# VectorE's program of a graph layer as one lap written out and two loops

## The reference

```
agg = segment_sum(edge_attr, dst, nodes)          # 200000 edges x 128, dst sorted, 6250 nodes
h   = relu(concat([x, agg, u], 1) @ W1 + b1)       # u: one row of 64, for all nodes
y   = x + h @ W2 + b2
out = (y - mean(y)) / sqrt(var(y) + 1e-5)          # over the 128 features of a node
```

## Time and profile before

| | us |
|---|---|
| median of 3 runs | 287.8 (287.53 to 287.91) |
| the profiled execution | 288.01 |
| its span, first to last instruction | 286.2 |
| outside the span | 1.8 |
| PE busy | 204.1 (71%) |
| DVE busy | 159.7 (56%) |
| ACT busy | 46.5 (16%) |
| POOL busy | 43.9 (15%) |
| bytes moved by DMA | 110.05 MB |

### The profile page before, as it was taken

One profiled execution on the slowest core, in us unless ns is written; L12 is line 12 of the kernel. 1 busy time (PEld: TensorE's weight loads), 2 busy tenths in 40 slices (PEclk: granted clock), 3 DMA queues, 4 the chain that ended last, 5 costly groups with the idle time before them and its releaser, 6 DMA issues.

```text
span 286.2 us, 11430 instructions
## 1 busy us (share of the span) xinstructions
PE 204.1 (71%) x4997; PEld 159.5 (56%) x4997; DVE 159.7 (56%) x422; ACT 46.5 (16%) x98; POOL 43.9 (15%) x49
## 2 busy tenths in 40 slices
PE   0567699786796697687946855956877668656782
PEld 0455587655575576566635644645555555545671
DVE  3983565764655754844864365274345454785522
ACT  0411032211220221212102101120111121110100
POOL 8200020210400400400421021040021040030020
PEclk9995999999999999999997999898979977997957
DMA  7999999999999999999999999999999999999991
GB/s 178 352 377 401 401 398 400 402 401 401 402 400 402 400 399 404 400 401 404 399 399 402 398 402 401 401 401 401 400 401 400 403 401 399 398 400 397 403 394 59
DMA packets 40092, 110.05 MB, mean 385 GB/s; under 512 B 2485, under 2 KB 3658, under 8 KB 40074
## 3 DMA queue, kind: packets, MB, share of 16 engines
q1 hardware_dynamic: 37012, 105.85, 95.9%
q10 hardware_dynamic: 3062, 3.99, 4.2%
HBM read 106.63 MB, written 3.20 MB: 384 GB/s over the span
## 4 chain that ended last, share of the span: by engine, by line
PE 47%; DMA 34%; issue 13%; DVE 3%; ACT 0%; SPq 0%; POOLq 0%; DVEq 0%; POOL 0%
DMA slots<-in_edge_attr 33%; PE rows_ps L738 26%; PE cols_ps L750 12%; PE hid_ps L782 2%; PE hid_ps L764 2%; DMA dst_int<-in_dst 2%; PE hid_ps L773 2%; PE hid_ps L758 1%; DVE low L505 1%; DVE edge_node L521 1%; PE rows_ps L723 1%; DVE z L608 0%; ACT rows L383 0%; PE hid_ps L858 0%; DVE dst_local L510 0%
## 5 line engine op out<-in xcount | busy, mean ns | idle before, releaser
L738 PE MATMUL rows_ps<-slots,hot 64*32 64x128 f32 (+1 forms) x4560 | 110.9, 286 | 59.3 <-issue 45.7
L738 PEld LDWEIGHTS rows_ps<-slots,hot 64*32 64x32 f32 (+1 forms) x4560 | 92.4, 112 | 76.0 <-issue 75.4
L570 DVE TENSOR_TENSOR agg_t<-agg_t,cols_ps 128x128 f32 (+1 forms) x65 | 21.7, 334 | 108.1 <-PE cols_ps L750 107.9
L551 DVE TENSOR_TENSOR hot<-edge_node,iota 128x768 f32<-128x768 f32 x65 | 61.9, 952 | 6.3 <-issue 6.3
L750 PE MATMUL cols_ps<-row_hot,rows 128*128 128x224 f32 (+1 forms) x190 | 48.5, 365 | 7.3 <-ACT rows L383 7.0
L383 ACT ACTIVATE rows<-rows_ps 128x128 f32<-128x128 f32 (+1 forms) x65 | 21.2, 326 | 190.7 <-PE rows_ps L738 186.9
L351 POOL TENSOR_TENSOR rstd<-var_eps,minus_half 128x4 f32<-128x4 f32 (+1 forms) x13 | 19.9, 1532 | 203.7 <-DVE var_eps L602 203.7
L750 PEld LDWEIGHTS cols_ps<-row_hot,rows 128*128 128x128 f32 x190 | 33.0, 200 | 21.5 <-ACT rows L383 12.8
L342 POOL TENSOR_TENSOR z<-x_rows,b_all 128x512 f32<-128x512 f32 (+1 forms) x13 | 16.2, 1250 | 35.5 <-PE hid_ps L758 35.2
L560 DVE TENSOR_TENSOR row_hot<-row_node,iota 128x448 f32<-128x448 f32 x30 | 19.6, 654 | 0.0
L608 DVE TENSOR_SCALAR z<-z,moments,rstd 128x128 f32<-128x128 f32 x49 | 18.6, 438 | 1.6 <-POOL rstd L351 1.6
(11 more groups left out here) (97 smaller groups left out, 65.4 us busy)
## 6 DMA issues: line engine op xcount, KB each, us to landing
slots<-in_edge_attr SPq DMA_DIRECT2D x65, 1536.0 KB, 18.6
x_rows<-in_x ACTq DMA_DIRECT2D x11, 256.0 KB
out<-z SPq DMA_DIRECT2D x11, 256.0 KB
dst_int<-in_dst SPq DMA_DIRECT2D x2, 192.0 KB, 4.2
dst_int<-in_dst ACTq DMA_DIRECT2D x2, 192.0 KB, 4.0
x_rows<-in_x ACTq DMA_DIRECT2D x1, 192.0 KB
out<-z SPq DMA_DIRECT2D x1, 192.0 KB
rest_slot<-in_edge_attr ACTq DMA_DIRECT2D x1, 160.0 KB, 8.8
```

The costliest lines, as they stand in the source:

```text
L551: V.tensor_tensor(hot[i][:, :, :], edge_node[:, bass.ds(t, 1), :, :].rearrange("p o c r -> p (o c r)").unsqueeze(2).broadcast_to([P, RUNS, ...
L570: V.tensor_tensor(cols, cols, cols_ps[:, 0:n], ALU.add).then_inc(added, 1)
L738: done = T.matmul(rows_ps[i][c * SPAN:(c + 1) * SPAN, h, 0:feats], hot[j][part, c * RUN + r, :], slots[part, j, c, r * feats:(r + 1) * fea ...
```

## The change

Only VectorE's program is written in another way. Lap 0 stays written out. Laps 1 to 5 become one loop (`Fori(1, DENSE_LAP)`) over `sparse_lap`, laps 6 to 12 a second (`Fori(DENSE_LAP, laps)`) over `dense_lap`. The lap's number is now a register, and so are addresses and wait values that hang on it. What only some laps do stands in `dve.If`:

- in a sparse lap, the `row_hot` for the steps t + 3 of j = 2, 3, 4 is the sparse or the dense form by two `If`, since those of lap 5 belong to lap 6;
- in a dense lap, `hot` and `row_hot` of j = 2, 3, 4 are made only where there is a lap to come; `judge` and `make_plan` stand in an `If` each.

`make_plan` stands now after `variance` of step j = 2 of the last lap; before, it stood at the end of step j = 1. `variance` waits at two places for `ids_copied` where its register form waited for `plan_made`; both are semaphores that have long been set where this is run. `edge_node` and `row_node` are longer by three steps, which are addressed but not used.

```diff
-        edge_node = sb("edge_node", [P, steps, TILES, RUN])
-        row_node = sb("row_node", [P, steps, HALVES])
+        edge_node = sb("edge_node", [P, steps + AHEAD, TILES, RUN])
+        row_node = sb("row_node", [P, steps + AHEAD, HALVES])
...
-                if dense_step:
+                make_row_hot(t, i, dense_step)
+
+            def make_row_hot(t, i, dense_step):
+                if dense_step is None:
+
+                    with dve.If(t < DENSE):
+                        make_row_hot(t, i, False)
+                    with dve.If(t > DENSE - 1):
+                        make_row_hot(t, i, True)
+                elif dense_step:
...
-                    dve.wait_ge(plan_made, 1)
+                    dve.wait_ge(ids_copied, CHUNKS)
...
-            def lap_of(lap):
-                at = step_bases(lap * LAP, LAP)
+            def counts(lap):
+
+                for j in range(-1, LAP + AHEAD + 1):
+                    dve.compute_val(lap * LAP + j)
+                for n in range(2):
+                    dve.compute_val(lap + n)
+                return step_bases(lap * LAP, LAP)
+
+            def sparse_lap(lap):
+                at = counts(lap)
                 for j in range(LAP):
                     t = lap * LAP + j
-                    if t + AHEAD < steps:
-                        make_hot(t + AHEAD, j + AHEAD, t + AHEAD >= DENSE)
-                    add(t, at[j], t >= DENSE)
-
-                    k = j + 1 if lap >= DENSE_LAP else j
-                    if lap and k == 2:
+
+                    mixed = not isinstance(lap, int) and j + AHEAD >= LAP
+                    make_hot(t + AHEAD, j + AHEAD, None if mixed else False)
+                    add(t, at[j], False)
+                    if isinstance(lap, int):
+                        continue
+                    if j == 2:
                         residual(lap - 1, lap - 1)
-                    elif lap and k == 3:
+                    elif j == 3:
                         variance(lap - 1, lap - 1)
-                    elif lap and k == 4:
+                    elif j == 4:
                         normalise(lap - 1, lap - 1)
-                    if t == (laps - 2) * LAP + 1:
-                        judge()
-                    elif t == (laps - 1) * LAP + 1:
-                        make_plan()
+
+            def dense_lap(lap):
+                at = counts(lap)
+                for j in range(LAP):
+                    t = lap * LAP + j
+                    if j + AHEAD < LAP:
+                        make_hot(t + AHEAD, j + AHEAD, True)
+                    else:
+                        with dve.If(lap < laps - 1):
+                            make_hot(t + AHEAD, j + AHEAD, True)
+                    add(t, at[j], True)
+                    if j == 1:
+                        residual(lap - 1, lap - 1)
+                        with dve.If(lap == laps - 2):
+                            judge()
+                    elif j == 2:
+                        variance(lap - 1, lap - 1)
+                        with dve.If(lap > laps - 2):
+                            make_plan()
+                    elif j == 3:
+                        normalise(lap - 1, lap - 1)
...
-            lap_of(0)
-            for lap in range(1, laps):
-                lap_of(lap)
+            sparse_lap(0)
+            with dve.Fori(1, DENSE_LAP) as lap:
+                sparse_lap(lap)
+            with dve.Fori(DENSE_LAP, laps) as lap:
+                dense_lap(lap)
```

## The result

The changed kernel is faster. Its median is 284.18 us (7 runs, 283.30 to 285.33), that of the kernel before, run beside it, 287.53 us (7 runs, 286.15 to 287.91). The ratio on record is 0.9916, 95% interval 0.9895 to 0.9937. It is not the quotient of the two medians, which would be 0.988: four of the seven times of the kernel before lie in an upper group near 287.8 us and three near 286.4 us, and its median falls into the upper one (more on this at experiments 10 and 11). The forecast was no change, 287.8 us, with 287.0 as the low end. The profiled execution took 284.0 us with a span of 282.3; before it was 288.0 with 286.2. So 3.9 us of the span have to be found.

A forecast was written before the change was run, and what follows sets the result against it. The prediction took the DMA transfers to bound the kernel. Its five terms were each 0, so 288.0 us stayed for an execution like the profiled one, 287.8 us for the median, range 287.0 to 289.0 us.

The forecast's parts named there:

- What bounds the kernel: Whole run: DMA transfers bound it, 276.1 us to the last landing, then 10.1 us of tail; VectorE has room.
- The register work: VectorE's loop laps: added branches and register instructions take 2.8 us sparse, 2.6 us dense, hidden in idle time; cost 0.
- the 2 us that I had allowed: Sign in the profile after: `level2`'s wait for VectorE's sums stays under 2 us in all.
- The waits and the last lap: VectorE's semaphore waits, and `make_plan` moved in the last lap: nothing new queued, flag ready near 273.5 us; cost 0.
- The tail: Behind the last load's landing: same VectorE instructions, the loop's last branch hidden in 1.60 us of waiting; cost 0.
- My sign for a wrong forecast: Last landing to the end: forecast wrong if this differs from 10.1 us by more than half a microsecond.
- The fetching of the program: Instruction packets on q14: some of ten go away, all 0.08 MB or 0.2 us at 401 GB/s; taken as 0.0.
- B: VectorE's dense loop is fetched anew at the branch back and the exit: 1.6 us slower, middle 289.0 us; chance 0.13.
- C: TensorE clock falls otherwise in the last step: at 2.4 GHz the tail loses 1.3 us, 286.5 us; chance 0.07.
- D: VectorE's branches dearer than any row: at 1.2 us each, DMA gaps and 301 us; chance 0.02.
- the 0.08 for shifts that I couldn't name: Landing or tail: unnamed small shifts beyond 0.6 us, half faster and half slower; chance 0.08.

The follow-up runs named there:

- experiments 10 and 11: Unaltered kernels run again: 10 the changed kernel, 284.24 us, ratio 0.9907; 11 the kernel before, 286.38 us, ratio 0.9995.
- second pair of profiles: The profiles from experiments 10 and 11, changed kernel and kernel before, both unaltered: spans 281.83 and 284.47 us.
- version 7: Changed kernel with a never-entered `If` around 600 `memset` in the first step of every dense lap: 314.76 us, ratio 1.1004.
- versions 8 and 9: Changed kernel with 106 and 122 waits (53 and 61 instructions) on VectorE ahead of the first lap: 285.05 and 285.23 us.
- version 4: Kernel before with 40 waits (20 instructions) at the start of each of ScalarE's laps: 286.37 us, ratio 1.0008.

## Why the prediction was wrong

**What bounds the kernel** was right and was read too coarsely. The transfers bound it, up to the last landing. But "the DMA" is sixteen lanes, and the sum of their rates, which the earlier trace rows show, says nothing of the one that ends last. In that view a lag of 3 us on one lane doesn't show: the 38th and 39th slice of before still have 403 and 394 GB/s.

**The register work** was right: hidden. Against one lap of before, VectorE's records of register instructions and branches grow by 1.8 us in the sparse lap and by 1.4 us in the dense lap of the stretches above, where I had 2.8 and 2.6, in 8.0 and 10.6 us of idle time. `level2` waited for sums 1.9 us in all (0.4 before), under the 2 us that I had allowed. The branch back is cheaper than I had it, 63 ns in the median where I took TensorE's 208, and no branch of VectorE in this trace took over 67 ns:

```profile
L705 DVEq COMPARE_BRANCH  x7: 50/63/63, 155.2 to 276.2; - x7
```

**The waits and the last lap** were right, at nothing. `make_plan` came even before the place that I gave it, at 270.0 to 270.8 and not at 273.5 (the sum behind it came earlier as well, at 272.24 and not at 275.55), and SP, which was the first to read the flag at 278.9, did so at 276.0:

```profile
L266 SPq TENSOR_LOAD <-plan x1: 534/534/534, 276.0 to 276.0; - x1
```

**The tail** was right in its instructions: the loop's last branch stands at 276.2, ahead of the 1.59 us of waiting before the residual, and the residual comes 1.88 us behind the sum, 278.01 less 276.13, where the earlier trace rows have 282.18 less 280.29. My sign for a wrong forecast was a stretch behind the last landing other than 10.1 us by over half a microsecond; it was 8.8, and it is 8.5 to 8.8 in all later profiles but those of versions 7, 8 and 9, the kernel before again included (8.5). So 1.3 of the 10.1 us that the sum started from belonged to one execution, whose last step had 0.53 of the clock.

**The fetching of the program** is the step that failed. That some of the ten packets go away was right. I priced them as bytes spread over all lanes: 0.08 MB at 401 GB/s, 0.2 us at most, and I took 0.0. That divides by sixteen what isn't shared by sixteen. What one packet costs is 0.9 to 1 us on one lane, and three went away (94, 201, 256 us, with those at 36 and 147 left). The last share's lag fell by 2.34 us, from 5.06 to 2.72, and the first share of that load came 0.28 us earlier, which makes the 2.6 us; in the second pair of profiles it is 2.56 and 0.08. It is less than three whole microseconds because VectorE's lane starts at another place in each execution: behind its first fetch it is 1.05 us behind the first share in before and 1.70 in the changed kernel. The row for this was there: the earlier trace rows have the packet at 94 us, and what had to be read next was not VectorE, which went on, but the load in flight.

**The rivals.** B did not occur: no fetch came a second time in a loop, and the exit at 280.4 took 0.54 us. Its mechanism is real, as versions 7, 8 and 9 show. At the end a stall at the branch over `general` alone cost 1.4 to 1.5 us in versions 8 and 9, where B had 0.6 for it. It needs a jump over a whole block. C came true in the first profile, for its 1.3 us; the kernel before shows it too, so it is luck in that comparison, and not what the ratio rests on. D is refuted by the 67 ns at most. No rival had the gain, and the 0.08 for shifts that I couldn't name was the only place for it.

Still open: why a packet of 0.34 us sets a lane back by 0.9 to 1 us, why VectorE's fetches go to the same lane each time, whether the clock at the end has anything to do with the landing, and which share of the cost in version 7 behind load 45 is VectorE's own standing still.

## What to carry to other kernels

Where transfers bound a kernel, look at the last of a transfer's sixteen landings and not at the mean rate; work that always hits the same lane adds up there, however few its bytes. Code that an engine runs through once is such work: fewer instructions on VectorE, by loops whose body fits in a few blocks, took 0.9% off a kernel in which VectorE has 40% idle time. Keep jumps shorter than a block near the end, and price a small clean gain against two profiles of the kernel before, since one of them may have an unlucky end.

## What the runs showed of the hardware

- A fetch of VectorE is one packet of 8 KB, 128 instructions, taking 0.34 us (128 from its count at the fetches, and from 260 added instructions that brought two more). It sets one and the same of the sixteen shares back by 0.9 to 1 us: 1.05, 2.02, 3.01, 4.08, 5.04 us behind after one to five of them. TensorE's packets, 16 KB, took 1.03 to 1.12 us, and the first four go with four other shares, each set back by 1.3 to 1.5 us. Two fetches of ScalarE set another share back by 0.5 and 0.7 us (at 82.9 us in before, at 123.5 in version 4).
- The lag isn't made up while the transfers follow one another without a gap (401 GB/s): 4.09 and 4.07 us in two loads that followed one another.
- VectorE keeps at least three blocks: a loop over three was fetched once. In a loop that skips over five, it fetched 4 to 5 times in most laps.
- VectorE's branch to a block that isn't there took 2.4 to 2.9 us, to one that is, 0.54 to 0.58. A loop's branch back is 63 ns in the median.
- The clock of TensorE at the end, 0.53 or 1.00 over the last step, differed between executions of the kernel before (2.79 and 1.52 us for the same 48 matmuls), and is worth 1.3 us.
